# The hand-over from attention to the mixture of experts: routing of the last half interleaved by hand with the shared products, sends without a gate on the products

## The chip, the cores and the metric

One core of one Trainium2 chip runs the whole program. The metric is the device time of one execution in microseconds (us). TensorE is called PE here, VectorE DVE, ScalarE ACT, GpSimd POOL and SyncE SP; SP only issues DMAs.

## The reference, cut to what matters

```python
x = L0_attn_hidden_states                       # 4 x 1024 x 256
x = _layernorm(x + _L0_attn_ref(x, ...))        # 16 query heads, 8 key heads, D = 128
x = _layernorm(x + _L0_ffn_ref(x, ...))

def _L0_ffn_ref(hidden_states, ...):            # E = 64 experts, F = 176, TOP_K = 6
    scores = softmax(x @ gate_w.T)
    topk_w, topk_idx = top_k(scores, 6)         # weights then divided by their sum
    # slot of a row = number of earlier rows that chose the same expert, capacity 768
    buf[expert, slot] = x[row]
    eo = (silu(buf @ w_gate) * (buf @ w_up)) @ w_down
    y[row] += eo[expert, slot] * weight
    return y + shared_swiglu(x)                 # FS = 352, for every row
```

The attention part is `y = (a @ v) / sum(a)` with `a = (q k / sqrt(128))**2 * exp(gate)` under a causal mask, and a projection with `Wc`.

## The kernel before

The 4096 rows are 4 batches of 1024. `schedule()` writes one list of tasks by hand; each engine's program walks this list and does its own part of every task, so the list is the order of each engine's queue, and semaphores join the queues. All matrix products of the reference are made of a high and a low part (three passes of `product()`, line L884; five passes of `down_passes()`, L893).

**Attention** goes by units: `score` (L884) and, three units later, `av` (L1260). The last two heads have 40 units of their own. After an `av` that ends a group come `normed` (DVE), `turn` (PE transposes L1273), `turn_lo`, `project` and `add` (DVE L1824) into `acc`.

**Routing** of a part of rows is the list `route_steps(p)`. `stat`, `std`, `norm` are the layer norm (DVE L1837 to L1855, with a square root on ACT); `store` writes the rows to DRAM; `x1t` turns 256 rows (PE L1304, ACT L1549, DVE L1862) and writes them to `x1t_dram`; `logit` is the product with the gate weights; `softmax0` needs an Exp on ACT; `softmax1`, `max`, `index` pick the six experts; `hot` and `chosen` (DVE L1898, L1906) make a 0/1 matrix; `count` (PE L1317 to L1324) counts earlier rows; `slots` (L1931 to L1936), `again` (L1898) and `send` (DVE L1942 to L1948) make slot numbers. Behind a `send` follow six `scatter` tasks of two indirect DMAs each (POOL L2189), which write 128 rows each into `slots`. The last batch is routed in two halves, parts 3 and 4, of 512 rows; a half has 24 of these DMAs. Steps of part 3 are done one at each unit from unit 20 of the last 40 on, and its last seven steps (`weight1` to `send1`) are left for the time behind attention.

**Shared products.** 16 jobs k (8 blocks of 512 rows, two jobs each): `gate_up(k, 0..2)` on PE, 18 matmuls, then `hidden(k, 0..3)` on ACT and DVE (L1573 to L1584, L1965 to L1973), and per block `shared_down` (40 matmuls of L893) into `y_e`, which `shared_out` writes to `y_part[0]`. `gate_up(k)` waits until `hidden(k-2)` has ended. Inputs come by `shared_in`: blocks 1 to 3 only when `attention_over` holds, that is, after the last `add`. `rank_keys` and `rank_experts` sort the experts by the rows that they got so far.

**Experts.** `SEQ` has 68 steps, 64 experts in pairs of a full and a less full one, and 4 short extra steps of 128 rows (`E`+0 to 3). Rows come by `rows_in` (L1100) and `extra_in` (L1105), weights by `raw_in` (L1071); `turn_x` (L1364), `gate_up`, `hidden`, `down`, ACT L1617, and then POOL adds each 128 rows into `y_part` by an indirect DMA (L2199). These are 234 adds.

**End.** After the last add, blocks of rows are loaded (`block_in`), summed on POOL (L2270), normalised (DVE L2112, ACT L1675) and stored. There are seven blocks of 4 x 128 rows and two of 2 x 128.

Of the kernel before, what the change touches and what calls it, by code (L numbers as in the profile page):

```python
# [55 lines left out]

OQ, OK, OC = 0, CC * R * D, CC * (R + 1) * D
# [27 lines left out]
NTH = {x_: i_ for i_, x_ in enumerate(MAINS)}  # L85
# [4 lines left out]
BLOCK_ROWS = [4] * (N // P // 4 - 1) + [2, 2]  # L90
# [64 lines left out]
SEND_FROM = 10, 28  # L155
# [18 lines left out]
def schedule():  # L174
# [131 lines left out]
    for u, (n_, g, s) in enumerate(UNITS_ALL):  # L306
# [91 lines left out]
    u = len(UNITS_ALL)  # L398


    first_up = [("gate_up", k, part) for k in range(2) for part in range(3)]
    while late:
        catch_up()
        do(*first_up.pop(0))
        run_late(u)
        u += 1
        if len(first_up) == 3:
            do("experts_begin",)
            for part in range(4):
                do("hidden", 0, part)  # L410
    catch_up()
    for task in first_up:
        do(*task)

    first, second = background, route_steps(B)
    assert [name for _, name in first] == ["weight1", "count", "slots", "again0", "send0", "again1", "send1"]
    to_x1t0, ahead_of_hot = 8, 13
    background = first[:3] + second[:to_x1t0]  # L420
    for step in second[to_x1t0:ahead_of_hot]:
        background += [step] + first[3:4]
        first[3:4] = []
    assert len(first) == 3 and background[-1][1] == "max"
    background += second[ahead_of_hot:]

    def route_some(count):
        while to_send:
            do(*to_send.pop(0))
        for _ in range(min(count, len(background))):  # L430
            route_step(*background.pop(0))
            while to_send:
                do(*to_send.pop(0))

    def hidden(k):
        for part in range(4):
            do("hidden", k, part)

    for m in range(1, XE):
        do("shared_in", m)  # L440
    route_some(3)
    do("rank_keys")

    do("gate_up", 2, 0)
    on_spare("rank_experts")
    route_some(2)
    for part in range(3):
        do("hidden", 1, part)
    route_some(1)
    do("hidden", 1, 3)  # L450
    route_some(3)
    do("gate_up", 2, 1)
    do("gate_up", 2, 2)
    do("gate_up", 3, 0)
    hidden(2)
    route_some(1)
    do("gate_up", 3, 1)
    route_some(2)
    do("gate_up", 3, 2)

    def shared_up(m):
        for k in (2 * m, 2 * m + 1):
            if k > 3:
                for i in range(3):
                    do("gate_up", k, i)
            if k > 2:
                route_some(paces[k])
                hidden(k)


    paces = [0, 0, 0, 3, 3, 3, 3, 3, 2, 3, 2]
    assert sum(paces) == len(background)
    paces += [0] * (2 * M - len(paces))
    for m in range(M):
        if m + 1 < M:
            shared_up(m + 1)
        for pair in range(MAIN // GROUP):
            on_spare("shared_down", m, pair)
        if m == M - 2:
            do("rows_in", MAINS[0])  # L480
            do("rows_in", MAINS[1])
        do("shared_out", m)
        if m + XE < M:
            do("shared_in", m + XE)
        if m < 2:
            do("raw_in", MAINS[m])
# [4 lines left out]
    assert not background and not to_send  # L491
    do("counted",)

# [13 lines left out]
    for place, x_id in enumerate(SEQ):  # L507
        k = 2 * M + place
# [1956 lines left out]
```

## Time and profile before

| | us |
|---|---|
| runs: median of 3 (lowest to highest) | 2260.99 (2257.62 to 2263.92) |
| profiled execution, its own time | 2278.41 |
| its span | 2276.6 |
| PE busy, share of the span | 94% |
| POOL busy | 33% |

The span is from the first to the last instruction. The page gives the busy share of each engine in 40 equal slices; the part that the change touches begins in slice 28 (1593 us):

```profile
PE   8999999999999999999999999999898899999980
```

An answer on waits or an order in time names behind `<-` what ended the idle time of an engine; `issue` there means that no semaphore event explains it.

### The profile page before, as it was taken

What the parts mean: (1) busy time and instruction counts of PE and PEld (TensorE: products, weight loads), DVE (VectorE), ACT (ScalarE), POOL (GpSimd) and SP (SyncE); (2) the same over time, 40 slices, a digit from 0 to 9 for tenths busy, and PEclk for the clock granted to TensorE, in tenths of its full rate; (3) what the DMA queues carried; (4) which work ended last, traced back from release to release, by engine and by line L of the source; (5) the groups of instructions that cost most, each with busy time, mean ns of one, the idle gap of its engine ahead of it and who ended that gap; (6) DMA issues with size and microseconds to landing.
All of it is one profiled execution on the core that took longest, in us unless ns stands there. A gap on an engine that the chain in (4) does not pass through costs nothing.

```text
span 2276.6 us, 38638 instructions
## 1 busy us (share of the span) xinstructions
PE 2143.7 (94%) x14567; PEld 1955.1 (86%) x14570; DVE 1281.2 (56%) x2838; ACT 1155.9 (51%) x2198; POOL 751.8 (33%) x750
## 2 busy tenths in 40 slices
PE   8999999999999999999999999999898899999980
PEld 6999998999889899888989898999687789999970
DVE  4444444454665445455644566545664678888853
ACT  4444545444444445444444444445333577778863
POOL 3121112100004510000452002530044478878885
PEclk9999999999999999999999999999999999999995
DMA  4876722122113311211331211322253789999957
GB/s 168 334 273 264 296 77 71 45 63 70 49 45 112 123 50 52 82 33 60 98 133 53 79 54 56 106 72 70 83 184 131 196 214 235 236 220 240 230 93 240
DMA packets 145924, 301.02 MB, mean 132 GB/s; under 512 B 20256, under 2 KB 82464, under 8 KB 145728
## 3 DMA queue, kind: packets, MB, share of 16 engines
q1 hardware_dynamic: 104240, 246.06, 32.4%
q0 software_dynamic: 41056, 51.96, 11.6%
q8 instruction: 117, 1.92, 0.3%
q14 instruction: 79, 0.65, 0.1%
q10 hardware_dynamic: 432, 0.44, 0.1%
HBM read 159.29 MB, written 142.67 MB: 133 GB/s over the span
## 4 chain that ended last, share of the span: by engine, by line
PE 82%; DVE 6%; ACT 4%; issue 4%; DMA 2%; POOL 2%; SPq 0%; another core or an unknown queue 0%; ACTq 0%; POOLq 0%; DVEq 0%
PE bank L884 50%; PE bank L1260 21%; PE bank L893 6%; PE bank L1273 2%; PE bank L1364 2%; DMA y_part<-y_e,row_token 1%; POOL y_part L2199 1%; DVE ub L1784 1%; DVE bank L1968 1%; ACT silu_b L1580 1%; DVE bank L1965 1%; DVE xe_lo L2042 0%; DVE stats L2112 0%; ACT q_hi L1507 0%; POOL slots L2189 0%
## 5 line engine op out<-in xcount | busy, mean ns | idle before, releaser
L1260 PEld LDWEIGHTS bank<-v,a 128*128 128x128 f32 x4608 | 603.9, 191 | 44.1 <-ACT a L1531 0.8
L1260 PE MATMUL bank<-v,a 128*128 128x129 f32 x4608 | 617.1, 275 | 0.6 <-ACT a L1531 0.6
L2199 POOL DMA_INDIRECT y_part<-y_e,row_token x234 | 360.2, 1539 | 128.3 <-issue 67.0
L2169 POOL TENSOR_TENSOR decay_all<-decay_all,tab 128x128 f32<-128x128 f32 x128 | 59.5, 465 | 918.5 <-DMA decay_all<-decay_dram 918.1
L1527 ACT ACTIVATE a<-bank,c_s 128x512 f32<-128x512 f32 x384 | 263.3, 686 | 181.0 <-PE bank L884 167.3
L1531 ACT ACTIVATE a<-ub 128x512 f32<-128x512 f32 (+1 forms) x256 | 133.8, 524 | 377.7 <-DVE ub L1784 355.2
L2189 POOL DMA_INDIRECT slots<-rows,slot_u x192 | 189.0, 985 | 315.9 <-PE bank L1260 140.5
L884 PE MATMUL bank<-q_hi,k_hi 128*128 128x512 f32 (+1 forms) x640 | 262.2, 410 | 8.3 <-DVE ub L1784 7.7
L1763 DVE TENSOR_TENSOR q_lo<-bank,q_hi 128x512 fp32r<-128x512 f32 x128 | 88.5, 692 | 272.5 <-ACT q_hi L1507 266.0
L884 PE MATMUL bank<-q_lo,k_hi 128*128 128x512 f32 (+1 forms) x640 | 237.8, 372 | 0.0
L884 PE MATMUL bank<-q_hi,k_lo 128*128 128x512 f32 (+1 forms) x640 | 236.7, 370 | 0.0
L884 PE MATMUL bank<-xe_hi,wf_hi 128*128 128x512 f32 (+8 forms) x504 | 192.6, 382 | 11.5 <-DMA xe_lo<-x1t_dram 5.0
L884 PE MATMUL bank<-xe_hi,wf_lo 128*128 128x512 f32 (+8 forms) x504 | 185.7, 368 | 3.5 <-issue 3.5
L884 PE MATMUL bank<-xe_lo,wf_hi 128*128 128x512 f32 (+8 forms) x504 | 185.9, 369 | 1.0 <-issue 1.0
L884 PE MATMUL bank<-xt_hi,w_hi 128*128 128x512 f32 x384 | 166.3, 433 | 2.4 <-DVE acc L1824 1.3
L884 PE MATMUL bank<-wc_hi,yt_hi 128*128 128x256 f32 x512 | 154.7, 302 | 2.9 <-DVE yt_lo L1814 2.9
L1824 DVE TENSOR_TENSOR acc<-bank,acc 128x512 f32<-128x512 f32 x128 | 88.1, 689 | 117.4 <-PE bank L884 116.2
L884 PE MATMUL bank<-xt_hi,w_lo 128*128 128x512 f32 x384 | 151.0, 393 | 0.0
L1784 DVE TENSOR_TENSOR ub<-bank,em 128x512 f32<-128x512 f32 (+1 forms) x256 | 140.8, 550 | 17.8 <-PE bank L884 8.7
L884 PE MATMUL bank<-xt_lo,w_hi 128*128 128x512 f32 x384 | 150.6, 392 | 0.0
L884 PE MATMUL bank<-wc_hi,yt_lo 128*128 128x256 f32 x512 | 145.0, 283 | 0.0
L884 PE MATMUL bank<-wc_lo,yt_hi 128*128 128x256 f32 x512 | 144.8, 283 | 0.0
(220 smaller groups left out, 4722.6 us busy)
## 6 DMA issues: line engine op xcount, KB each, us to landing
slots<-acc SPq DMA_DIRECT2D x64, 816.0 KB, 7.9
w_raw_f<-in_wffn SPq DMA_DIRECT2D x66, 624.0 KB
decay_all<-decay_dram SPq DMA_DIRECT2D x128, 128.0 KB
xr<-slots SPq DMA_DIRECT2D x18, 544.0 KB
xr<-slots SPq DMA_DIRECT2D x20, 476.0 KB
w_hi<-w_dram SPq DMA_DIRECT2D x24, 384.0 KB
w_lo<-w_dram SPq DMA_DIRECT2D x24, 384.0 KB
sum<-y_part SPq DMA_DIRECT2D x14, 512.0 KB, 10.0
```

Source lines behind the costliest of these rows:

```text
L884: ins = e.matmul(dst, a, b, start=first and i == 0, stop=last and i == len(passes) - 1, skip_group_check=True)
L893: ins = e.matmul(dst, a, b, start=first and n_ == 0 and p_ == 0, stop=n_ == len(steps) - 1 and p_ == len(passes) - 1, skip_group_check=True)
L1260: ins = e.matmul(dst[:, tt, r, :], a32[u % NA][:, r, t0:t0 + P], v[n % 3][:, s, :], start=(s == 0 and r == 0), stop=(s == 2 * g + tt), ski ...
L1273: ins = e.transpose(ps[:, r, tt * P:(tt + 1) * P], yn[j % YR][:, tt, r, :], ident)
L1527: e.activation(squares, score_bank(u)[:, 0:R * w].rearrange("p (r t) -> p r t", r=R), ACT.Square, scale=c_s[b % 2][:, g * (g - 1) + s, h:h ...
L1531: e.activation(squares, ub[masked_nth[u] % 2][:, :, 0:w], ACT.Square).then_inc(s_sq)
L1763: e.tensor_tensor(lo, bank[6 + m % 2][:, :], f32(hi), ALU.subtract).then_inc(s_out_of[m % 2])
L1784: e.tensor_tensor(ub[mine % 2][:, :, 0:w], score_bank(u)[:, 0:R * w].rearrange("p (r t) -> p r t", r=R), decay.unsqueeze(1).to_broadcast([ ...
L1824: e.tensor_tensor(part, bank[6 + m % 2][:, :].rearrange("p (t c) -> p t c", c=C), part, ALU.add).then_inc(s_out_of[m % 2])
L2169: e.tensor_tensor(arg[:, GROUP:GROUP + P], arg[:, P:GROUP], mask, ALU.add)
L2189: e.indirect_dma_start(out=slots, out_offset=bass.IndirectOffsetOnAxis(ap=slot_u[:, j, k:k + 1], axis=0), in_=rows[:, j, :], in_offset=Non ...
L2199: e.indirect_dma_start(out=y_part[part], out_offset=bass.IndirectOffsetOnAxis(ap=token, axis=0), in_=y_rows, in_offset=None, bounds_check= ...
```

## The change

1. In the last 20 units of attention the steps in `TOGETHER` no longer take a unit each: `stat0` and `stat1` share one, `norm0`, `norm1`, `store` and `x1t0` share one, and so on. All 27 steps of part 3 fit, its sends' slot numbers too.
2. Behind attention the steps of part 4 stand at places written out by hand between parts of `gate_up` and `hidden`. `stat` waits for the projection of its own 256 rows only.
3. `scatter` no longer waits for a count of shared products (`SEND_FROM`).
4. `extra_in(E)` is issued behind block 6's `shared_out`, `rows_in(MAINS[1])` and the other three `extra_in` behind block 7's, all ahead of `raw_in(MAINS[2])`. `rank_counts` and `load_count` stand at expert step 8 instead of 2.
5. The end has eight blocks of 4 x 128 rows, in other buffers.
6. Tasks for late shared blocks (`late_in`, `late_down`) are added, but `M1 = 8` makes `ML = 0`, so that none of them is made.

```diff
+M1 = 8
+ML = M - M1
-BLOCK_ROWS = [4] * (N // P // 4 - 1) + [2, 2]
+BLOCK_ROWS = [4] * M1 + [2] * (2 * ML)
-SEND_FROM = 10, 28
+TOGETHER = ("stat0", "norm0", "norm1", "store", "softmax1", "chosen_bf", "weight0")
...
             route_step(p, name)
+            while p == B - 1 and name in TOGETHER:
+                p, name = background.pop(0)
+                route_step(p, name)
...
+    catch_up()
+    up(0, 0)
+    do("experts_begin")
+    send_all()
+    hidden(0, 0)
+    up(0, 1)
+    on_spare("turn", HEADS - 1, NG - 1)
+    do("turn_lo", HEADS - 1, NG - 1)
+    up(0, 2)
+    hidden(0, 1)
+    on_spare("project", HEADS - 1, NG - 2)
+    hidden(0, 2)
+    up(1, 0)
+    do("add", HEADS - 1, NG - 2)
+    on_spare("project", HEADS - 1, NG - 1)
+    hidden(0, 3)
+    route_to("stat0")
+    up(1, 1)
+    do("add", HEADS - 1, NG - 1)
     for m in range(1, XE):
         do("shared_in", m)
+    route_to("std")
+    up(1, 2)
+    hidden(1, 0)
+    route_to("store")
+    up(2, 0)
+    route_to("x1t0")
+    hidden(1, 1)
+    up(2, 1)
+    route_to("logit0")
+    hidden(1, 2)
+    route_to("x1t1")
+    up(2, 2)
+    hidden(1, 3)
+    route_to("logit1")
     do("rank_keys")
+    shared_end(0)
     on_spare("rank_experts")
+    do("raw_in", MAINS[0])
+    route_to("softmax0")
+    up(3, 0)
+    hidden(2, 0, 1)
+    route_to("softmax1")
+    up(3, 1)
+    route_to("max")
+    up(3, 2)
+    hidden(2, 2, 3)
+    route_to("index")
+    up(4, 0)
+    route_to("chosen0")
+    up(4, 1)
+    hidden(3, 0, 1)
+    up(4, 2)
+    route_to("chosen1")
+    hidden(3, 2, 3)
+    shared_end(1)
+    do("raw_in", MAINS[1])
+    route_to("weight1")
+    hidden(4, 0, 1)
+    up(5, 0)
+    route_to("count")
+    hidden(4, 2, 3)
+    up(5, 1)
+    route_to("slots")
+    route_to("send0")
+    up(5, 2)
+    hidden(5)
+    route_to("send1")
...
+        if m == M1 - 2:
+            do("rows_in", MAINS[0])
+            do("extra_in", E)
+    do("rows_in", MAINS[1])
+    for i in range(1, EXTRA):
+        do("extra_in", E + i)
...
-        if place == 2:
+        if place == 8:
             on_spare("rank_counts")
             do("load_count")
...
-                    n, g, j0 = b * H + H - 1, (t0 + nt - 1) // 2, t0 + 2 * int(name[4:])
+                    n, j0 = b * H + H - 1, t0 + 2 * int(name[4:])
+                    g = j0 // 2
...
                 once.wait_ge(s_av, sent_behind["scatter", p, q, piece])
-                if PARTS[p][0] == B - 1:
-
-                    once.wait_ge(c_gu, SEND_FROM[p - B + 1] + (q * SENDS + piece) * 5 // 4)
```

`route_to(name)` does the steps of part 4 up to `name` and each send's DMAs behind it; `up` is `gate_up`; `shared_end(m)` is the two `shared_down`, `shared_out(m)` and `shared_in(m + 4)`.

## Rows read from the trace of the kernel before

**Rows 1.** Busy time by stage: us, PE, PEld, DVE, ACT, POOL, clock, DMA, GB/s.

```profile
1635.00:1700.00 65.00, 57.12 (x281) 47.65 (x282) 39.89 (x85) 25.82 (x42) 23.88 (x24) 0.86 0.50 172
...
1700.00:1768.00 68.00, 59.62 (x343) 50.31 (x342) 34.41 (x58) 25.53 (x46) 23.75 (x24) 0.92 0.41 136
...
1853.00:2205.00 352.00, 351.56 (x2341) 326.97 (x2340) 293.40 (x647) 277.91 (x572) 288.91 (x188) 1.00 0.93 217
...
2205.00:2240.00 35.00, 3.65 (x29) 3.20 (x27) 1.15 (x2) 3.45 (x9) 25.36 (x19) 0.62 0.45 50
```

**Rows 2.** Groups of GpSimd by line, 1853 to 2238 us: xcount, busy, mean, idle.

```profile
L2199 POOL DMA_INDIRECT y_part<-y_e,row_token x205 | 315.3, 1538 | 72.3 <-issue 60.3 <-DMA y_part<-y_e,row_token 9.2 <-ACT y_e L1617 1.8
```

**Rows 3.** GpSimd in order of time: start, us, engine, line, idle before it.

```profile
1787.41 1.59 POOL L2199 DMA_INDIRECT y_part<-y_e,row_token  x1 [40.41 <-DVE rank_over L2012]
```

**Rows 4.** Who TensorE waited for, 1600 to 1830 us: total, times, longest.

```profile
PE bank L884 <- issue: 5.0, 5, 1.7
...
PE bank L884 <- DMA xe_lo<-x1t_dram: 5.0, 1, 5.0
...
PE bank L884 <- DVE hb L1973: 4.4, 2, 3.3
...
PE bank L893 <- issue: 4.2, 5, 1.7
...
PE bank L1364 <- DMA xo<-slots: 4.2, 1, 4.2
...
PE bank L884 <- DVE x1t_lo L1862: 1.1, 1, 1.1
```

**Rows 5.** Chain of work, 1585 to 1830 us: start, us, what.

```profile
1747.79 8.30 PE bank L884 x36
...
1756.09 9.61 PE bank L893 x80
```

**Rows 6.** Groups of VectorE by line, 1633 to 1702 us.

```profile
L1898 DVE TENSOR_TENSOR onehot<-chosen_at,tab 128x768 f32<-128x768 f32 x4 | 3.8, 954 | 0.1
...
L1906 DVE TENSOR_REDUCE chosen<-onehot 128x128 f32<-128x768 f32 x2 | 3.0, 1518 | 0.1
...
L1942 DVE TENSOR_TENSOR onehot<-onehot,slot_of 128x384 f32<-128x384 f32 x4 | 2.0, 553 | 0.0
...
L1946 DVE TENSOR_REDUCE slot_f<-onehot 128x12 f32<-128x768 f32 x2 | 1.9, 953 | 0.1
```

**Rows 7.** The same chain where attention ends, 1620 to 1640 us.

```profile
1621.79 1.28 ACT L1573
...
1623.08 0.61 ACT silu_a L1573
...
1627.80 1.30 DVE acc L1824 x2
...
1629.73 5.17 DMA xe_lo<-x1t_dram
```

**Rows 8.** Sends on GpSimd, and TensorE's gaps beside them.

```profile
L2189 POOL DMA_INDIRECT slots<-rows,slot_u x48 | 47.6, 992 | 77.2 <-DVE slot_u L1948 38.7 <-PE bank L884 23.2 <-issue 12.5
...
1660.83 1.01 POOL L2189 DMA_INDIRECT slots<-rows,slot_u  x1 [38.68 <-DVE slot_u L1948]
...
1675.26 0.28 PE L893 MATMUL bank<-wf_hi,ha_lo 128*128 128x256 f32 x1 [1.73 <-issue]
...
1711.69 0.97 POOL L2189 DMA_INDIRECT slots<-rows,slot_u  x1 [15.29 <-PE bank L884]
...
1726.81 0.39 PE L884 MATMUL bank<-xe_lo,wf_hi 128*128 128x512 f32 x1 [1.02 <-issue]
```

**Rows 9.** SyncE's issues where the expert stage begins.

```profile
1767.55 0.37 SPq L1071 DMA_DIRECT2D w_raw_f<-in_wffn  x1
...
1770.21 3.69 SPq L1105 DMA_DIRECT2D xo<-slots  x4
```

**Rows 10.** ScalarE's last instructions.

```profile
2272.08 2.06 ACT L1675 ACTIVATE sum<-sum,row_rec,rstd 128x256 f32<-128x256 f32 x4
```

More of the change, by code:

```diff
@@ L84 @@
 REST = 4
-NTH = {x_: i_ for i_, x_ in enumerate(MAINS)}
+W_ORDER = MAINS + (list(LATE) if ML else [])
+NTH = {x_: i_ for i_, x_ in enumerate(W_ORDER)}
+KX = 2 * M1
+KL = KX + STEPS
+KR = KL + 2 * ML
 PLACE = {x_: i_ for i_, x_ in enumerate(SEQ)}
-BLOCK_ROWS = [4] * (N // P // 4 - 1) + [2, 2]
+BLOCK_ROWS = [4] * M1 + [2] * (2 * ML)
 DT = max(BLOCK_ROWS)
@@ L397, in schedule @@
                 do("x_rest", b1, x_split_at.index(at))
[L398 to L427, printed above, removed]
+    assert not background
+    second = route_steps(B)
+    tail = [item[1:] for item in late]
@@ L428, in route_some, with send_all, route_to @@
+    assert tail == [("project", HEADS - 1, NG - 2), ("turn", HEADS - 1, NG - 1), ("project", HEADS - 1, NG - 1)], tail
+    def send_all():
         while to_send:
             do(*to_send.pop(0))
[L430 to L436, printed above, removed]
-            do("hidden", k, part)
+    def route_to(name):
+        while True:
+            p, step = second.pop(0)
+            route_step(p, step)
+            send_all()
+            if step == name:
+                return
@@ new lines, in up, with hidden, shared_end @@
+    def up(k, *parts):
+        for part in parts or range(3):
+            do("gate_up", k, part)
+    def hidden(k, *parts):
+        for part in parts or range(4):
+            do("hidden", k, part)
+    def shared_end(m):
+        for pair in range(MAIN // GROUP):
+            on_spare("shared_down", m, pair)
+        do("shared_out", m)
+        if m + XE < M1:
+            do("shared_in", m + XE)
+    catch_up()
+    up(0, 0)
+    do("experts_begin")
+    send_all()
+    hidden(0, 0)
+    up(0, 1)
@@ L456, in schedule @@
[L456 to L467, printed above, removed]
-                hidden(k)
[L471 to L486, printed above, removed]
+    do("raw_in", MAINS[0])
@@ L487, in schedule @@
+    route_to("send0")
+    up(5, 2)
+    hidden(5)
+    route_to("send1")
+    assert not second
+    for m in range(2, M1):
+        if m + 1 < M1:
+            for k in (2 * m + 2, 2 * m + 3):
+                up(k)
+                hidden(k)
+        shared_end(m)
         if m in (2, 3):
@@ L507, in schedule @@
     for place, x_id in enumerate(SEQ):
-        k = 2 * M + place
-        later = MAINS[NTH[x_id] + 2:NTH[x_id] + 4] if x_id < E else []
-        if later:
+        k = KX + place
+        later = W_ORDER[NTH[x_id] + 2:NTH[x_id] + 4] if x_id < E else []
+        if later and later[0] >= 0:
             do("rows_in", later[0])
-        if place == 0:
-            for i in range(EXTRA):
-                do("extra_in", E + i)
-        if place == 2:
+        if place == 8:
             on_spare("rank_counts")
@@ L519, in schedule @@
             do("raw_in", later[1])
-        do("gate_up", k, 0)
-        do("hidden", k, 0)
+        up(k, 0)
+        hidden(k, 0)
         if place + 1 < STEPS:
@@ L542, in schedule @@
             down(SEQ[place - 1], (1,))
-    down(SEQ[-1], (0, 1))
+        if ML and place == STEPS - 2:
+            do("late_in", 0)
+    if not ML:
+        down(SEQ[-1], (0, 1))
+    for d in range(ML):
+        for k in (KL + 2 * d, KL + 2 * d + 1):
+            up(k)
+            hidden(k)
+            if k == KL:
+                down(SEQ[-1], (0, 1))
+        if d + 1 < ML:
+            do("late_in", d + 1)
+        for pair in range(MAIN // GROUP):
+            on_spare("late_down", d, pair)
     return order, spare
@@ L838, in build @@
         c_x = [signal(f"c_x{i}") for i in range(XE)]
+        c_late = [signal(f"c_late{i}") for i in range(2)]
         c_r = [signal(f"c_r{i}") for i in range(XS)]
@@ L1103, in extra_in @@
                 all_sent(once)
-                once.wait_ge(c_gu, 3 * 2 * M)
+                once.wait_ge(c_gu, 3 * 2 * (max(m for m in range(M1) if m % XE > 1) + 1))
                 e.dma_start(xo[x_id - E][:, :, :], rows_at(expert_at(x_id), MAIN, 1, P)).then_inc(c_extra[x_id - E], 16)
@@ L2110, in block_stats @@
                 once.wait_ge(d_sum, n + 1)
+                if n >= M1:
+                    d, pair = divmod(n - M1, MAIN // GROUP)
+                    once.wait_ge(*out_of(("late_down", d, pair)))
+                    step(e.tensor_tensor(sum0[n], sum0[n], y_e[late_y(d)][:, 2 * pair:2 * pair + 2, :], ALU.add))
+                    steps_done()
                 for j in range(BLOCK_ROWS[n]):
```

133 lines of the change are left out of this document (81 added, 52 removed).

## The prediction, made before the changed kernel was run

> **What bounds the kernel now.** First the stages [rows 1], since the change touches only the hand-over between attention and experts, and the end. Read PE's busy share against the clock column there. In 1635 to 1768 us PE is busy for 116.7 of 133 us, and at a mean granted clock of 0.86 and 0.92: part of this busy time is at the lower level of 1.2 GHz. From 1853 to 2205 us it is busy for 351.6 of 352 us at the full clock. Then POOL by line [rows 2]: its 205 adds there take 1.54 us each, and of their 72.3 us of idle time 60.3 are "issue", 0.3 us ahead of each. That is 1.84 us per add and nothing left over. PE ends at about 2210 us, POOL adds until 2236 (the last stage of [rows 1]). So from 1853 us on POOL's adds set the end, and the only way in which the hand-over can change the time is that the first add, now at 1787.4 [rows 3], comes earlier or later. What POOL waits for between its first adds and 1853 us are mostly landings of earlier adds; these are of the adds' own order and move along.
>
> What PE waited for in the hand-over [rows 4]: 5.0 us once for the inputs of shared blocks 1 to 3, 4.4 us in two waits for `hidden` on DVE, 9.2 us (5.0 + 4.2) in ten "issue" gaps, 1.1 us for `logit0`, 4.2 us for the rows of the first extra expert. The chain [rows 5] prices the undisturbed work: 36 matmuls, two jobs, take 8.30 us, 4.15 a job; 80 of L893, two blocks, take 9.61 us, 4.8 a block.
>
> **The change part by part.** Times are those of the profiled execution. It took 2278.41 us, 17.4 above the median of the runs; I carry the difference over to the median unchanged.
>
> *Attention's last 20 units, +0.7.* With `x1t0` in the unit of `norm0` and `norm1`, PE meets it directly and waits for the chain square root (its table load is priced by the one of ACT L1573, 1.28 us [rows 7]), reciprocal and four `norm` instructions, in all about 2 us behind PE. A wait of 0.8 us at today's `logit0` and one of 0.6 us go, because the load for the next Exp no longer stands ahead of `x1t`. The two-part lumps on DVE (`stat0` with `stat1`, `chosen_bf` with the weights) come between masked products that have slack. `count` adds no PE work, it moves. Bounds 0 and +2.5.
>
> *Part 3's sends inside attention, +2.7.* Between the last masked product and the last `normed` and `turn_lo`, DVE today does `hot1`, `chosen1`, `chosen_bf` and `weight0`: 0.95 + 1.52 [rows 6] + about 0.8 = 3.3 us. Afterwards it does `again0`, `send0`, `again1`, `send1`: each pair is 0.95 (L1898) + 2 x 0.51 (L1942; its mean of 553 ns holds an overlap) + 0.95 (L1946) + 0.2 = 3.1 us [rows 6], 6.3 us in all. The difference is 3.0; `slots` in place of `chosen0` one unit earlier gives 0.3 back. This is on the path: DVE runs from here without a pause to the last `add`, behind which `shared_in(1..3)` are issued, and their landing 5.2 us later [rows 7] is what PE waits for. The first of them leaves at 1629.1 today, at about 1631.8 afterwards, and PE begins job 2 at about 1638 instead of 1634.9. Bounds 0 (DVE has more slack than counted) and +4 (18 sends that now share the DMA engines with these 3 MB).
>
> *The interleaved steps of part 4, +2.0.* Now the 5 us wait is filled on DVE with `stat`, `std`, `norm`: `x1t0` runs at about 1641 instead of 1647. I followed the new list in order with today's durations, and found three waits of PE for `hidden`. (a) DVE's queue has `rank_experts` behind `shared_end(0)`, so it stands still until PE has done 40 matmuls (4.8 us). Only then come `softmax0`, ACT's Exp with one table load, and job 2's Silu with another: 0.9 + 1.3 + 0.4 + 1.3 + 0.6, then `hidden(2)` with `softmax1` and `max` in between, 4.7. That is 9.2 us, while PE has the 4.15 us of job 3: `gate_up(4)` waits about 4.6 us (the sum gives 5.0; some of it overlaps). (b) `chosen0` and `chosen1` with their `hot` steps, 2 x 2.5 us [rows 6], stand ahead of `hidden(3)`: PE waits about 2.2 us before `shared_down(1)`. (c) `slots`, `again0`, `send0` (4.2 us) stand ahead of `hidden(5)`: about 4.0 us before `gate_up(7)`. The sum is 10.8 against 4.4 and 1.1 [rows 4] today, +5.3. Against it stand the "issue" gaps. They occur only beside POOL's sends, and begin about 12 us after a burst of them does: burst from 1660.8, gaps from 1673.5; burst from 1711.7, gaps from 1724 [rows 8]. Part 3's burst, which made 3.3 us of them, now lies mostly where PE waits anyway: -3.3. Part 4's (5.9 us) I leave as it is. The half-clock stretches behind the waits I take as equal. Bounds -8 (all gaps go, with the slow stretches behind them) and +12 (see the rival below).
>
> *The first experts, -2.0.* The extra expert's rows are issued at 1770.2 today [rows 9] and PE waits 4.2 us for them [rows 4]; issued a block earlier they are there. But what was ahead of them falls behind: `raw_in(MAINS[2])`, today at 1767.55 [rows 9], now has `rows_in(MAINS[1])` and three `extra_in` ahead of it on SP, and four of these take 3.69 us plus the last one's way, some 1.1 us each, so 4.7 us later. ACT's `split_hi` of these weights stands ahead of `hidden(16, 1)`, waits for them and returns about 2.2 us of the gain. Bounds -4.2 and 0. `load_count` at step 8 comes before POOL is full; 0, bounds -0.5 and +1.
>
> *The end, +0.7.* One block of four instead of two of two: the same bytes and sums, one chain fewer, but the last `out` has 512 KB and the last norm is four instructions of 0.5 us instead of two [rows 10], +1.0, less 0.3 for a pass through three engines. Bounds 0 and +1.5.
>
> Without a gate, `scatter` waits on nothing new. Behind it on POOL are only `experts_begin` and the adds, which come 60 us later.
>
> Sum: +0.7 + 2.7 + 2.0 - 2.0 + 0.7 = **+4.1 us**, a span of about 2281 us, and 2260.99 + 4.1 = **2265** for the median.
>
> The Trainium skill (ScalarE: Activation LUTs, What ACT_TABLE_LOAD costs) adds a drain of about 1.4 us to every load of about 1.28 us. The trace has the load with 1.28 us, and Silu began 0.01 us after it [rows 7], so it does not agree about the drain here. By the page, the two loads in (a) would cost 2.8 us more, and this change, which puts them on PE's path, would end near 2268.
>
> **The rivals.** *Faster: the hand-written order does what it is written for.* My following of the list is a chain of some sixty instructions; if DVE reaches each `hidden` before PE asks, the waits (a) to (c) are not there, and neither are those of today (-4.4 and -1.1), the issue gaps shrink by 6, and about 4 us of half-clock work behind them go: -15.5, with +2.7, +0.7 and +0.7 as above and the first experts at -2.0: -13, **2248**. For it: DVE is busy for only 39.9 of 65 us and 34.4 of 68 us [rows 1], so there is room for any order. Against it: room in the sum is not room ahead of `hidden(2)`, where three engines take turns.
>
> *Slower: the gate paced the sends, and without it both bursts are longer.* Today the 48 sends wait 23.2 us for PE [rows 8], that is, at the gate, which cuts them into bursts of 12 to 16. Unpaced, at 0.99 + 0.3 us each, part 4's 24 last 31 us and part 3's last 18 last 23 us. If gaps run from 12 us on to the burst's end, with today's share of idle time of 0.56 (6 of 10.7 us), that makes 19 x 0.56 = 10.6 and 11 x 0.56 = 6.2 us instead of 5.9 and 3.3, and the second already counted as gone: +4.7 + 6.2 = +10.9, with half-clock stretches of some 2 us behind: 2265 + 12 = **2277**. It decides from a burst longer than about 12 us on. For it: no gap of this kind stands elsewhere [rows 4]. Against it: what stops PE in them is not shown, and a load ended in both bursts just before them.
>
> The Trainium skill (Runtime: NRT & Kernel Launch, Instruction fetch mechanics) has instruction blocks fetched ahead by DMA, the fetch hidden. No row here says whether a fetch made these gaps; the page speaks against that and for no longer gaps.
>
> *No effect at all: the end is POOL's.* If the first add moves but POOL's early waits take it up, **2261**. Against it: those waits are for landings of its own adds.
>
> **How the numbers follow.** This kernel's measurements tell about 0.3% (6.8 us) from no change. My own case, +4, has 0.38 (together with its slower neighbours up to +7 and its faster ones down to -4); no effect 0.08; the faster rival 0.26, nearly all of it beyond -0.3%; the slower one 0.20; the order costing more than I counted (the table drain, a fourth wait) 0.08, also beyond +0.3%. Hence faster 0.26, same 0.44, slower 0.30, some of my own case lying beyond +0.3% too. The range 2246 to 2279 reaches to both rivals' values.
>
> **What the profile would show.** Last `add` of attention and `shared_in` 2 to 3 us later after the last L1260; waits of PE for L1973 before jobs 4 and 7, and before the second L893 block; no wait for `xo`, but one of ACT L1564 for a load at the first expert; issue gaps near the end of the second burst; 205 adds at 1.84 us from 1853 on. The prediction is wrong if DVE waits nowhere for `rank_experts`, if the issue gaps follow neither burst, or if the first add's shift is not the end's.

## The result

The changed kernel takes 2282.3 us, the median of four runs; the kernel before took 2261.95 in the same comparison. The ratio is 1.0089 (95%: 1.0069 to 1.011): 20 us slower, where +4 had been forecast. Its profiled execution, one of these four, took 2279.0 us and has a span of 2277.3. The span of the kernel before was 2276.6; its profiled execution (2278.4 us) is none of the timed ones, which took 2257.6 to 2263.9. So the two profiles differ by 0.7 us, and the timed runs by 20. That is the first thing to explain.

Where the rows of before stood, the changed kernel has these. Stages (us, PE, PEld, DVE, ACT, POOL, clock, DMA, GB/s), for [rows 1]:

```profile
1635.00:1700.00 65.00, 49.97 (x227) 41.29 (x228) 35.63 (x78) 18.45 (x32) 17.77 (x19) 0.79 0.48 169
1700.00:1768.00 68.00, 64.38 (x398) 56.98 (x397) 31.02 (x51) 30.91 (x53) 17.11 (x17) 1.00 0.40 131
```

Whom PE waited for in the changed kernel, 1575 to 1775 us (total, times, longest), for [rows 4]:

```profile
PE bank L936 <- DVE hb L2066: 9.2, 3, 4.6
PE bank L936 <- DMA xe_lo<-x1t_dram: 7.7, 1, 7.7
PE bank L936 <- DVE x1t_lo L1955: 3.6, 1, 3.6
PE bank L1375 <- DVE rows L1948: 3.2, 1, 3.2
PE bank L1448 <- DMA xr<-slots: 2.1, 1, 2.1
PE bank L945 <- DVE hb L2066: 1.9, 1, 1.9
```

The last products of attention, and the first add, for [rows 3]:

```profile
1612.28 0.71 PE L1331 MATMUL bank<-v,a 128*128 128x129 f32 x4 [0.34 <-ACT a L1615]
...
1784.78 1.58 POOL L2294 DMA_INDIRECT y_part<-y_e,row_token  x1 [62.64 <-ACT y_e L1709]
```

Read three things. From 1635 to 1700 us PE is busy for 50.0 us where it was 57.1, at a granted clock of 0.79 instead of 0.86. There is no "issue" row: the gaps of [rows 4] are gone. And the stretch from the last products of attention to the first add is 172.5 us long; in the trace of before it was 171.5 (1615.91 to 1787.41). That stretch is the measure in what follows, because the time from the first add to the end of the span changes less from kernel to kernel: it is 489 to 497 us in all traces here.

Where the changed kernel's attention ends, its chain of work (start, us, what) goes over POOL's sends:

```profile
1623.04 0.97 POOL slots L2284
1625.39 0.57 POOL hb L2291
1626.04 0.60 ACT hb L1668
...
1627.38 0.75 DVE stats L1930 x2
1628.13 0.60 DVE acc L1916
1628.75 0.57 SPq L1145
1629.37 5.91 DMA xe_lo<-x1t_dram
1635.32 2.93 PE bank L936 x6
```

`experts_begin` zeroes `hb` on POOL, and six of part 3's sends stand ahead of it. ACT's `hb` waits for it, DVE's `hidden(0)` for ACT, and behind that stand the last `add` and the loads of the shared blocks.

### The profile page after: what moved, and what is told of

Read it like the earlier page. It is cut to its first block, busy times and chain, and to the rows that moved or that the text cites. A ratio compares the mean times of both kernels' runs of the same rounds, so it can differ in the third digit from the quotient of the medians.

```text
span 2277.3 us, 38627 instructions
## 1 busy us (share of the span) xinstructions
PE 2139.7 (94%) x14567; PEld 1957.7 (86%) x14570; DVE 1277.9 (56%) x2835; ACT 1155.9 (51%) x2197; POOL 751.0 (33%) x749
## 4 chain that ended last, share of the span: by engine, by line
PE 80%; DVE 6%; ACT 4%; issue 4%; DMA 3%; POOL 2%; SPq 0%; ACTq 0%; POOLq 0%; DVEq 0%
PE bank L936 49%; PE bank L1331 21%; PE bank L945 6%; PE bank L1344 2%; DMA y_part<-y_e,row_token 2%; PE bank L1448 1%; POOL y_part L2294 1%; DVE ub L1876 1%; DVE bank L2058 1%; DVE bank L2061 1%; ACT silu_b L1664 0%; POOL slots L2284 0%; ACT wf_hi L1648 0%; DVE xe_lo L2135 0%; ACT y_e L1709 0%
```

## Experiments

Kernels measured one after the other on one chip, the kernel before among them, make a session here. Comparisons are by the ratio to the kernel before in the same session, because its median is not the same in all of them. The numbers behind a ratio, in brackets, are its 95% interval.

### Undoing and doing the parts one by one

**b_end.** Only the end: `BLOCK_ROWS = [4] * (N // P // 4)`.

> The kernel before with the end alone changed: eight blocks of four rows of tiles instead of seven and two halves; everything up to the last add is as before. Two questions. The end by itself: my step had +0.7 us, bounds 0 and +1.5. And the profiled execution of the kernel before, which took 2278.4 us where its timed runs took 2261. Theory A: that execution was not like the timed ones; its ten 'issue' gaps of PE (9.2 us between 1673 and 1734 us) and the half-clock work behind them are absent in most executions. Then this profile, of the same hand-over, shows few or none of them, a first add near 1772 us instead of 1787, and an execution of about 2262 us. Theory B: the gaps belong to the kernel before, and profiling lengthens every execution of it by some 17 us: then the gaps stand here again and the profiled execution is near 2278 us.

Measured: 2264.94 us against 2264.51, ratio 1.0005 (0.999 to 1.002). Its profiled execution took 2265.6 us, and has no "issue" row at all. PE's waits in it, 1575 to 1775 us:

```profile
PE bank L884 <- DVE hb L1973: 6.4, 3, 3.7
PE bank L884 <- DMA xe_lo<-x1t_dram: 5.0, 1, 5.0
PE bank L1364 <- DMA xo<-slots: 3.5, 1, 3.5
PE bank L884 <- DVE x1t_lo L1862: 2.0, 2, 1.2
```

and its two ends of the hand-over:

```profile
1614.90 0.71 PE L1260 MATMUL bank<-v,a 128*128 128x129 f32 x4 [0.62 <-ACT a L1531]
...
1771.81 1.59 POOL L2199 DMA_INDIRECT y_part<-y_e,row_token  x1 [35.55 <-DVE rank_over L2012]
```

The hand-over code is that of before, but the stretch is 156.9 us instead of 171.5. So theory A holds: the profiled execution that I had read belonged to another condition than the timed runs. Against this base the changed kernel's 172.5 is 15.6 us worse, and its profiled execution 13.4 us longer (2279.0 against 2265.6): most of the 20 us can be seen in the traces.

**b_nogate.** Only the gate: the line `once.wait_ge(c_gu, SEND_FROM[...] + ...)` in `scatter` goes.

> The kernel before with one wait less: the last half's indirect sends no longer wait for a count of gate_up parts (c_gu), only for their slot numbers. If the unpaced sends are the cause of the 20 us (they crowd the transfers that PE waits for), this alone is slower by 8 to 20 us, about 2270 to 2282 us. If the cause is what was moved (part 3 finished inside attention, or the hand-written order), this is within 3 us of the kernel before, 2258 to 2265 us. My prediction's slower rival had +12 us for it through 'issue' gaps.

Measured: 2264.22 us, 1.0000 (0.9983 to 1.0017), stretch 156.2 us. Without the gate this kernel is the same within 0.2%.

**b_part3.** Only part 3's steps in attention, with what belongs to them: no gate for its sends, and `stat` waits for its own 256 rows.

```diff
+            while p == B - 1 and name in TOGETHER:
+                p, name = background.pop(0)
+                route_step(p, name)
...
-    first, second = background, route_steps(B)
+    first, second = [(B - 1, None)] * 7, route_steps(B)
```

> The kernel before with one change: part 3's last seven steps (weight1 to send1) are done inside attention as in the changed kernel, and part 3's sends have no gate; part 4's steps keep their old places, the old first seven places stay empty, and part 4's sends keep their gate. If the loss comes from part 3 in attention (its sends stand ahead of the zeroing of hb on POOL, its slot arithmetic ahead of the last add on DVE, and its 24 sends beside the loads of shared blocks 1 to 3), most of the 20 us is here: 2272 to 2282 us. If it comes from the hand-written order or the unpaced sends of part 4, this is 2258 to 2266 us. My own step had +3.4 us (0.7 + 2.7) for it less 3.3 for gaps.

Measured: 2266.51 us, 1.0015 (1.0001 to 1.0029), stretch 158.6 us. PE waits 7.5 us for the shared blocks instead of 5.0, and restarts 22.9 us after the last products of attention (1614.33 to 1637.23) instead of 19.0 (1614.90 to 1633.91); of these 3.9 us the stretch keeps 1.7. In time the ratio is worth 3.4 us, between 0.2 and 6.6.

**a_gate4.** The changed kernel with `if p == B: once.wait_ge(c_gu, 28 + (q * SENDS + piece) * 5 // 4)` put back.

> The changed kernel with the gate back for part 4's sends alone (gate_up count from 28 on, as before). If unpaced sends of part 4 cost the time, this gains 5 us or more on the changed kernel's 2282, to 2277 or less. If not, it stays within 3 us, or is somewhat slower, because the last sends of 24 then end at about 1745 us instead of 1722.

Measured: 2281.81 us, 1.0081 (1.0056 to 1.0105), stretch 173.1 us. The unpaced sends are not the cause where there are no gaps; this trace and the changed kernel's have none.

**allbut_again** and **a_again**, in one session: everything but the hand-written order (b_part3, no gate, the loads of b_extra, `load_count` at step 8, b_end), and the changed kernel itself. Between the two stand the hand-written order, from the end of attention on, and the other buffers of the end.

> The kernel of b_allbut again (the whole change but the hand-written order), which was at 1.006 on a chip with the 'issue' gaps, where its 24 sends ran unbroken for 31 us and had 12.6 us of gaps beside them. On a chip without them: 1.000 to 1.003 if the hand-written order is what costs the changed kernel its 0.9%, 1.006 or more if the other parts together do. On a chip with them: 1.006 again, and the changed kernel's ratio less this one is the order's price.

> The changed kernel itself, for a comparison on the same chip with the other three. The kernel before took 2264.5 us on the chip of b_end, b_nogate, b_part3 and a_gate4, whose traces have no 'issue' gaps of PE beside the sends, and 2279.8 us on that of b_allbut, b_extra, a_rank and a_held, whose traces all have them. Theory: a chip has them or not. On one without, the changed kernel is at 1.008 to 1.009 of the kernel before and its trace has no gaps; on one with them, gaps begin about 12 us after the first of its 24 unpaced sends of part 4 and last until they end, some 19 us with 11 to 14 us of gaps, and the ratio is above 1.009.

Measured: 1.0007 (0.9997 to 1.0018) and 1.0065 (1.0048 to 1.0082). **The order costs 0.58%, 13 us; all the rest together 0.07%.** The stretch is 160.5 us (1615.93 to 1776.44) against 172.9 (1615.16 to 1788.05), 12.4 us more. The 20 us of the first comparison (its interval is 16 to 25) were 14 here (11 to 19); where the rest of them was I can't say. PE's waits with the old order:

```profile
PE bank L890 <- DMA xe_lo<-x1t_dram: 7.5, 1, 7.5
PE bank L890 <- DVE hb L1980: 3.8, 2, 3.0
```

and with the hand-written one:

```profile
PE bank L936 <- DVE hb L2066: 9.2, 3, 4.6
PE bank L936 <- DMA xe_lo<-x1t_dram: 8.0, 1, 8.0
...
PE bank L945 <- DVE hb L2066: 1.9, 1, 1.9
```

For `hidden` that is 11.1 us against 3.8: 7.3 us of the 12.4. The remaining 5.1 are for the most part slower work. From the last products of attention to the first add, first allbut_again, then a_again:

```profile
1616.60:1776.44 159.84, 136.72 (x754) 117.39 (x754) 89.78 (x183) 62.39 (x109) 49.38 (x53) 0.90 0.50 169
```

```profile
1615.90:1788.05 172.15, 141.41 (x755) 120.88 (x756) 89.42 (x183) 63.45 (x109) 49.41 (x53) 0.88 0.47 157
```

PE does the same products (754 and 755 are recorded), but is busy for 141.4 us instead of 136.7, 4.7 more, at a mean clock of 0.88 instead of 0.90. How such work looks in a chain, here the changed kernel's, with the same line at both levels:

```profile
1651.06 6.68 PE bank L945 x40
...
1694.23 6.77 PE bank L936 x18
1701.01 4.79 PE bank L945 x40
1705.80 8.30 PE bank L936 x36
```

Block 0's products took 6.68 us where the next block's took 4.79, job 7's 6.77 where 4.15 is a job's undisturbed time (half of 8.30). The old order has such rows too. In allbut_again block 0's products are even slower:

```profile
1662.09 7.52 PE bank L899 x40
```

So single rows against full speed don't price the new order; the difference of the two sums, 4.7 us, does.

### What is late in the hand-written order

**a_rank.** `rank_experts` and `raw_in(MAINS[0])` moved from behind `shared_end(0)` to behind `hidden(2)`.

> The changed kernel with rank_experts (and raw_in(MAINS[0]), which needs its result) moved from behind shared_end(0) to behind hidden(2): DVE no longer stands still until PE has done the 40 products of shared block 0 before it can begin softmax0. Theory of my step (a): the wait of 4.6 us before gate_up(4) comes from there; it goes, or falls under 1 us, and with it some of the half-clock work behind it (2.6 us in gate_up(4)), and the kernel gains 5 to 7 us, to about 2276. Rival: softmax0's chain over ACT with its two table loads is late anyway; the wait stays above 3 us and the time within 2 us of the changed kernel's.

Measured: PE's wait before `gate_up(4)` is 4.71 us; in the changed kernel it is 4.63. ACT's rows in that trace say why:

```profile
1663.65 0.60 ACT L1690 ACTIVATE y_e<-bank 128x512 f32<-128x512 f32 x1 [8.05 <-PE bank L945]
1666.24 0.60 ACT L1690 ACTIVATE y_e<-bank 128x512 f32<-128x512 f32 x1 [1.99 <-PE bank L945]
1666.86 1.28 ACT L1637 ACT_TABLE_LOAD   x1
1668.15 0.42 ACT L1637 ACTIVATE shifted<-shifted 128x256 f32<-128x256 f32 x1
1668.59 1.28 ACT L1657 ACT_TABLE_LOAD   x1
1669.88 0.60 ACT L1657 ACTIVATE silu_a<-bank 128x512 f32<-128x512 f32 x1
```

DVE had `softmax0` ready at 1661.8, but on ACT the two `y_e` copies of `shared_end(0)` stand ahead of the Exp, and ACT waits there for PE's 40 products. My cause was the wrong queue, or rather one of two: in a_again, without the edit, DVE stands at `rank_experts` until 1660.56, and ACT's first copy begins at 1660.39, so both are held by the same 40 products, and freeing DVE alone gains nothing. The kernel took 2310.58 us, 1.0139 (1.0103 to 1.0175); this and its stretch of 198.8 us are from a session with "issue" gaps (below), beside no run of the changed kernel, and give no verdict on the edit. PE waited 9.7 us in it for `x1t_lo`, beside part 3's sends, where a_held, without sends there, waits 1.2. The sends alone are not the reason, since with the same sends it waits 2.9 in b_allbut, measured in the same session, and 3.2 in a_again; what made it 9.7 I haven't found.

**a_act.** The same place mended on ACT:

```diff
-    shared_end(0)
-    on_spare("rank_experts")
-    do("raw_in", MAINS[0])
     route_to("softmax0")
+    hidden(2, 0)
+    shared_end(0)
     up(3, 0)
-    hidden(2, 0, 1)
+    hidden(2, 1)
+    on_spare("rank_experts")
+    do("raw_in", MAINS[0])
```

> The changed kernel with softmax0 and the first part of hidden(2) ahead of shared_end(0), and rank_experts behind hidden(2)'s second part. Moving rank_experts alone (a_rank) left PE's wait before gate_up(4) at 4.70 us, and its trace showed why: on ACT the two y_e copies of shared block 0 stand ahead of softmax0's Exp, and ACT waited 8.1 and 2.0 us for PE's 40 products there. Theory: that is the cause of wait (a); with Exp and Silu ahead of these copies the wait falls under 1 us and the kernel gains 4 to 7 us, with the half-clock work behind it. Rival: something else is late next, the wait only moves to shared_down(1) or gate_up(7), and under 2 us are gained.

Measured: the wait before `gate_up(4)` falls from 4.6 to 1.5 us, but the one before `shared_down(1)` rises from 1.9 to 4.3. The stretch is 169.8 us, 3.1 less. The time is 2281.32 us, 1.0068 (1.0053 to 1.0083), beside a_again's 1.0065: no gain that can be told. The theory had the cause, the rival the effect.

**a_mend.** All three: as a_act, `hidden(3)` ahead of `chosen0`, `hidden(4)` ahead of `chosen1`, `hidden(5)` ahead of `slots` and the sends.

> The changed kernel with all three waits for hidden mended: as a_act, and hidden(3) ahead of chosen0, chosen1 behind hidden(4), slots and the sends behind hidden(5). If the hand-written order costs by these waits and the half-clock work behind them, PE's 10.4 us in them fall under 2 us, about 5 us of half-clock time go too, and the kernel is 10 to 15 us faster than the changed one, about 1.003 of the kernel before on a chip without gaps; what remains is part 3 in attention. If it costs in another way, less than 6 us are gained.

Measured: 2282.05 us, 1.0060 (1.0041 to 1.0080). The waits for `hidden` fall from 11.1 to 7.1 us and the stretch to 166.9. But in this execution attention ended at 1621.1 instead of 1615.2, and the six microseconds gained were lost there. Its five executions took 2274.3 to 2283.1 us, and the traced one is the longest of them; whether the others lost the same is not known. The stage where that happened, first a_again's, then a_mend's:

```profile
1580.00:1600.00 20.00, 16.43 (x121) 15.00 (x120) 12.80 (x42) 10.94 (x18) 0.00 (x0) 1.00 0.24 80
```

```profile
1580.00:1600.00 20.00, 16.84 (x96) 15.64 (x95) 11.29 (x33) 7.74 (x13) 0.87 (x2) 0.74 0.24 81
```

The same products in the same order, the same 3.2 us wait for `rows` just before them, and 96 done instead of 121, at a mean clock of 0.74 instead of 1.00. Why the clock fell behind this wait in one kernel and not in the other isn't shown. The instructions up to there are the same. It was 0.74 or 0.75 in a_held, a_mend and both runs of a_best, and 0.91 to 1.00 in all others.

**a_held.** Part 3's sends all behind `experts_begin`, with their old gate.

> The changed kernel with part 3's sends all behind experts_begin on POOL and gated again by the count of gate_up parts (from 10 on, as before), while its slot arithmetic stays in attention. It tells what these sends cost where they are now: the zeroing of hb waits for six of them (ACT waits 3.4 us for it), and the 3 MB of shared blocks 1 to 3 and the write of x1t land beside 18 of them (PE waits 7.7 us and 3.6 us). If they cause it, PE's wait for xe_lo falls from 7.7 to about 5, the wait for the x1t write from 3.6 to under 1, and 3 to 6 us are gained. If the waits come from DVE's slot arithmetic alone, less than 2 us is gained.

Measured: PE waits 4.9 us for the loads instead of 7.7 to 8.0, and 1.2 for the write of `x1t` instead of 3.2 to 3.6. It restarts 20.3 us after the last products of attention (1617.46 to 1637.75) instead of the changed kernel's 23.0 (1612.28 to 1635.32). So the sends, and not DVE's slot arithmetic, are most of what part 3 costs there: 2.7 of the 4.0 us by which the changed kernel restarts later than b_end (19.0 us). The time, 2298.86 us and 1.0082 (1.0055 to 1.0110), has 15 us of "issue" gaps in it, of the kind below.

### The "issue" gaps

**b_extra** (the kernel before, with the loads of the extra experts' rows ahead of `raw_in(MAINS[2])`) and **b_allbut**, the same kernel as allbut_again, ran in a session in which the kernel before took 2279.78 us.

> The kernel before with one change: rows_in of the first expert behind shared_out(6), the first extra expert's rows behind it, rows_in of the second and the other three extras behind the last shared block, all of them ahead of raw_in(MAINS[2]). My step had -2.0 us for it (bounds -4.2 and 0): PE's wait of 3.5 to 4.2 us for xo goes, ACT waits for raw_in in its place. In the changed kernel's trace two waits stand where I had one: 2.1 us for xr (its load is now behind shared_out(6) on SP) and 4.3 us ahead of the first down rows. If those come with this change alone, it gains nothing or loses up to 3 us; if they come from the order, it gains 2.

> The changed kernel in everything but the hand-written order of part 4's steps and of the shared products: part 3 finished in attention, no gate, the extra experts' rows a block earlier, load_count at step 8, eight equal blocks at the end; part 4's steps at the old kernel's paces, the places of the seven steps that went left empty. Theory now: the hand-written order costs nearly all of the 20 us, and the rest some 2 us in all: 2262 to 2269 us. Rival: parts that cost nothing one by one cost together, or the earlier rows of the extra experts cost: 2275 us or more.

Measured: b_extra 0.9994 (0.9976 to 1.0013), its stretch 171.0 us. PE's wait for `xo` is gone, and one of 2.4 us for `xr` and one of 3.2 at the first `down` have come: both are this part's, not the order's. b_allbut 1.0060 (1.0042 to 1.0078), the very kernel that was at 1.0007 in the session above. Its first send of part 4, the first two gaps beside the 24, and the sum of its waits by "issue":

```profile
1712.34 0.99 POOL L2193 DMA_INDIRECT slots<-rows,slot_u  x1 [62.02 <-DVE slot_u L1955]
...
1725.36 0.28 PE L899 MATMUL bank<-wf_hi,ha_lo 128*128 128x256 f32 x1 [1.02 <-issue]
1726.79 0.28 PE L899 MATMUL bank<-wf_hi,hb 112*128 112x256 f32 x1 [1.15 <-issue]
...
PE bank L890 <- issue: 9.3, 8, 1.7
PE bank L899 <- issue: 4.0, 3, 1.9
```

The gaps begin 12.0 us after the burst does (1712.34 to 1724.34) and last until 2 us after its end. One of the eleven rows, 0.7 us at 1621, is not of this kind: it stands in attention, where the other kernels wait 0.7 us for `yt_lo`. The ten beside the sends sum to 12.6 us. Beside part 3's 18 sends, unbroken for 22.7 us in the same trace, there is none, though PE waits there for other things part of the time. allbut_again has none beside the same 24 sends. Both ran on one chip, at different times.

**b_spread**: the gate's values alone, `SEND_FROM[p - B + 1] + (q * SENDS + piece) // 4 * 6`.

> The kernel before with the gate's values alone changed: bursts of 8 sends (about 10 us), each released 6 gate_up parts after the one before, instead of a task of two sends every 1.25 parts. In a session with the 'issue' gaps: none or nearly none, if the length of a burst makes them (they began 12 us into one), and then 9 us of gaps and the half-clock work behind them go, 0.993 to 0.996; if sends as such make them, the gaps are as before and the ratio 1.000. In a session without gaps the ratio is 1.000 either way, and it tells only that this pacing costs nothing.

Measured, in a session with gaps (kernel before 2280.09 us): 2284.55 us, 1.0024 (1.0011 to 1.0037). The bursts ran together, to 16, 8, 16 and 8 sends. The gaps begin 12.7 and 12.1 us into the two of 16, last until 2.5 us after their end, and sum to 14.7 us:

```profile
PE bank L893 <- issue: 12.8, 11, 1.9
...
PE bank L884 <- issue: 1.9, 3, 0.8
```

Beside the two bursts of 8, 10 us long, there is none.

**b_rank**: `on_spare("rank_experts")` ahead of `do("gate_up", 2, 0)`. **b_best**: b_rank, b_spread's gate, the first extra's rows ahead of `shared_out(7)`, `slots` a job earlier.

> The kernel before with two lines exchanged: the product of rank_experts ahead of gate_up(2, 0) on PE. In b_end's trace DVE stood 5.0 us at rank_experts, whose product was queued on PE behind gate_up(2, 0) and so behind the load that PE waits 5 us for; hidden(1) is behind it on DVE, and PE then waits 3.7 us for hidden(1) ahead of gate_up(3). Theory (a wait in the hand-over moves the first add and the end by its length): PE's 3.7 us go, the wait of 1.2 us at logit0 shrinks, the first add is 4 us earlier, the time 0.1 to 0.2% less, 0.998 to 0.999. Rival: x1t0 then waits for the write of its own tile or PE falls to half clock elsewhere: within 0.05%.

> The kernel before with b_rank, b_spread, the first extra expert's rows issued ahead of shared_out(7) and still ahead of raw_in(MAINS[2]), and part 4's slots step one job earlier (PE's wait of 2.3 us before gate_up(11)). Theory: 3.7 + 1.2 + 2.3 us in the hand-over and 3.5 us for xo go, 8 to 10 us, 0.995 to 0.997 without gaps in the session, below 0.992 with them. Rival: what is removed returns behind the next load (xr, raw_in) or as half-clock work: 0.998 to 1.000.

Measured: b_rank 2275.27 us, 0.9981 (0.9966 to 0.9996), its stretch 168.8 us against 171.5 and 171.0 in the two other traces of this hand-over with gaps: a wait of some 3.7 us taken out at its cause gave back 0.19%, 4 us (1 to 8). Its first long burst is a case against the 12 us. It has 14 sends and lasts from 1665.98 to 1684.06, and its only gaps (one more "issue" row is explained below) are 1.3 us from 1684.5 on, after its last send:

```profile
1665.98 0.97 POOL L2189 DMA_INDIRECT slots<-rows,slot_u  x1 [2.60 <-PE bank L884]
...
1685.37 0.28 PE L893 MATMUL bank<-wf_hi,ha_lo 128*128 128x256 f32 x1 [0.85 <-issue]
```

b_best 0.9996 (0.9977 to 1.0014), where below 0.992 was expected: its bursts of 16 have 12.4 us of gaps, from 12.7 us into the first and from 16.0 us into the second. Its stretch is 167.3 us, 4 less than before, and the time from its first add to the end is 494 us where the kernel before has 489; what took the gain there I haven't followed.

**a_best**: a_mend's order, part 3's sends behind `experts_begin`, bursts of 8 that stay apart, the loads as in b_best.

> The changed kernel with a_mend's order, all of part 3's sends behind the zeroing of hb, both parts' sends gated in bursts of 8, and the loads of the first experts' rows as in b_best. If the waits and the transfers beside the sends are all that the hand-written order loses, this is within 0.2% of the kernel before or faster, 0.997 to 1.002, with 155 to 160 us from the last av product to the first add. If the order loses in a way that I have not found, it stays at 1.004 or more.

Measured, in the same session: 2269.23 us, **0.9953** (0.9937 to 0.9969), stretch 156.9 us. PE's waits in its trace, 1575 to 1775 us, have one row by "issue" left:

```profile
PE bank L943 <- DVE hb L2073: 4.7, 3, 2.6
...
PE bank L943 <- issue: 1.1, 1, 1.1
```

and even this is a wait for `hidden`: PE goes on right behind DVE's `hb`, and the same kernel in a session without gaps (a_best2) has a fourth wait for `hb`, of 1.1 us, at this place (5.8 us in four instead of 4.7 in three).

```profile
1682.31 0.68 DVE L2073 TENSOR_TENSOR hb<-bank,hb 48x512 fp32r<-48x512 f32 x1
...
1683.05 0.50 PE L943 MATMUL bank<-xe_hi,wf_hi 128*128 128x512 f32 x1 [1.12 <-issue]
```

The same is true of one row each in a_held (4.0 us), b_rank (2.3) and b_best (0.6), which are not counted as gaps here.

**b_short** (the kernel before with the gate at 10, 19, 26 and 33, 38, 44) and **a_best2**, the kernel of a_best, in a session without gaps:

> The kernel before with the gate's values alone changed, to three bursts of 8 sends for each part, released at gate_up counts 10, 19, 26 and 33, 38, 44, so that in its trace some 3 us lie between them. b_spread's bursts ran together to 16 sends, 20 us, and had 14.7 us of gaps, all from 12 us into a burst on; a_best's bursts of 8 had 1.1. Theory: a burst must last over 12 us to stop PE. In a session with gaps: under 2 us of gaps instead of 9, and 0.994 to 0.997 of the kernel before. In a session without: 0.999 to 1.001.

> The kernel of a_best again (mended order, part 3's sends behind the zeroing, bursts of 8, the first experts' rows as in b_best), 0.9953 in a session with gaps. In a session without gaps nothing is left for the bursts to gain: 0.998 to 1.001 if the mended hand-over is as good as the old one, where the changed kernel was 1.0065 to 1.0089. In a session with gaps 0.995 again, and within 0.2% of b_short if the bursts are what gained.

Measured: b_short 1.0022 (1.0009 to 1.0035); its bursts are of 8, but the last send ends at 1745 instead of 1736 us, and PE waits 1.7 us for the first rows, whose load waits for all sends. Its stretch is 157.6 us; the larger part of its loss, 5 us from the first add to the end, I haven't followed. a_best2 1.0016 (1.0001 to 1.0030), stretch 156.2 us. Without gaps to save, the mended order is as fast as the old one from attention's end on (156.2 against 156.9 us). What it loses lies ahead of that: in its trace attention ended at 1621.5, in b_short's at 1614.8, with the slow stage that a_mend has. So a_best beats the kernel before where the gaps are and is 0.16% behind it where they are not; the changed kernel, 1.0065 to 1.0089 without gaps, was not run with them. Whether short bursts alone end the gaps in the kernel before wasn't shown: b_short met none.

## The prediction, step by step

**The base of the sum.** I added +4.1 us to a profiled execution of 2278.41 us and carried the 17.4 us to the median over unchanged. This step failed. Most of the 17.4 us were the "issue" gaps and what goes with them: the stretch is 171.5 us in that trace and 156.9 in the same hand-over without gaps, 14.6 less. They were part of what the change touches, and so they could not be carried over. In the changed kernel's profiled execution they aren't there; that is why the sum against its own profile (+4.1, measured +0.7) looks right and the median is off by 17 us. The sign was in the material: the profile was 0.8% above three runs that agreed within 0.3%, and the one thing in it that I could not explain stood in the stages that were being changed.

**The interleaved steps, +2.0.** This is the term that was mis-sized: it measured +12.4 us in the stretch and 13 in the time. The new waits were right: 4.6, 2.2 and 4.0 us forecast, 4.6, 1.9 and 3.9 found, with a fourth of 0.7. Three things around them were wrong. The old order in company of the rest of the change waits 3.8 us for `hidden`, and I had 5.5 with `logit0` to set against 10.8: +7.3 instead of +5.3. The 3.3 us of gaps that I credited did not exist in the timed runs. And "the half-clock stretches behind the waits I take as equal" was worth about 5 us: with the longer waits the same products kept PE busy for 4.7 us more, at a lower mean clock. The cause of wait (a) was also wrong: with `rank_experts` out of the way (a_rank) the wait stays, because ACT's `y_e` copies hold the Exp; I had followed DVE's queue past `shared_end(0)` and not ACT's. That 4.6 us came out all the same was luck: the same 40 products hold both queues.

**Part 3 in attention, +0.7 and +2.7.** Right in the sum, in part by luck: b_part3 is at +0.15%, 3.4 us, with an interval of 0.2 to 6.6. PE waited 3.2 us for `rows`, not 2, and restarted 3.9 us later, not 3.1. The reason was for the larger part another one. I had priced DVE's slot arithmetic at 2.7 us; with the sends held back (a_held) PE restarts only 1.3 us later than in b_end, and the sends, which I had only in a bound, cost the other 2.7. "Behind it on POOL are only `experts_begin` and the adds, which come 60 us later" is wrong for `experts_begin`: it stands behind six sends and is on the chain (ACT waits 3.4 us for it). And the 3 MB and the `x1t` write beside 18 sends land later: 5.91 and 6.29 us, where b_end has 5.15 for the first and a_held 3.56 for the second.

**The first experts, -2.0.** b_extra gives -0.06% (-0.24 to +0.13), which holds -2.0 and 0 alike. The `xo` wait went, as forecast. In its place came ACT's wait for `raw_in`, which was forecast (2.2 us; 1.7 in b_extra and 2.0 in the changed kernel), and one for `xr`, which wasn't: its load now stands behind `shared_out(6)`, which waits for the copies of that block. The changed kernel's first add comes 2.6 us before that of [rows 3], but this compares one trace with gaps to one without.

**The end, +0.7; the end is POOL's.** b_end: +0.05% (-0.1 to +0.2). From the first to the last add it is 446 to 454 us in every trace, so the first add's shift is for the most part the end's.

**The rivals.** The faster one fell: DVE's spare time in the sum was not there ahead of `hidden`. The slower one, longer bursts with gaps, had the size about right where gaps exist: in b_allbut 12.6 us of them for the 19 us that its burst lasts beyond the twelfth, a share of 0.66 against the 0.56 that I used, and this kernel is at 1.0060 with gaps and at 1.0007 without, 12 us. Its rule, gaps from 12 us on to the burst's end, does not hold in all traces (b_rank, b_best). And it is not what made this result: the changed kernel's trace has no gap, and b_nogate and a_gate4, in a session without gaps, show nothing for the gate. The Trainium skill (Runtime: NRT & Kernel Launch, Instruction fetch mechanics) was set against that rival; nothing measured here says whether a fetch has to do with the gaps. On the table loads the Trainium skill (ScalarE: Activation LUTs, What ACT_TABLE_LOAD costs) has a drain of about 1.4 us; in a_rank's rows the next instruction begins 0.01 us after each load of 1.28, so the trace again doesn't agree.

## What to carry to other kernels

Before a sum is made against a profile, ask whether the profiled execution is one of the timed ones. If it is longer than they are, look for what could be the difference in the stages that the change touches, and make the sum with it and without it.

When steps are interleaved by hand, follow the list on every engine past each task that waits for the bottleneck: here a `shared_end` held not only DVE's queue, which I had followed, but ACT's too, with the next Exp and Silu behind it. A wait that is added costs its length and, behind it, work at the lower clock: here some 5 us for 7.

## What the hardware showed

The "issue" gaps of PE come with the session, not with the kernel or the chip: one chip had them in all four traces at one time (kernel before 2279.8 us) and in none of four at another (2265.8 us). With them, most bursts of 12 to 24 indirect sends (15 to 31 us) stop PE again and again, from 12 to 16 us after their start until up to 3.5 us after their end, for 6 to 15 us in a trace; beside bursts of 8 sends (10 us) there was none. The length of a burst does not decide alone: one of 14 sends, 18 us long, had 1.3 us of gaps at its end (b_rank), and one of 18, 22.7 us long, had none (b_allbut). What stops PE there is open. In such a session a_best, with short bursts, does 0.6% better against the kernel before than without gaps (0.9953 and 1.0016).
